# Sparse expert layer by scatter to expert regions and register-addressed block loads, and attention's output projection in plain fp32

## The chip, the cores and the metric

One Trainium2 chip, one core of it. The metric is device time in microseconds (us) of the whole kernel, one launch. In the profile PE is TensorE (matmuls; PEld its weight loads), DVE is VectorE, ACT ScalarE, POOL GpSimd, SP SyncE, which issues the plain DMAs.

## What is computed

Two layers on `x` of 4 sequences x 256 tokens x 256 values. Each layer adds an attention part and a feed-forward part, each on a layer-normed x and scaled by the tanh of a gate. The change touches the second layer only:

```python
# attention, 16 heads, scores against kv_r (4 x 256 x 64)
ctx_c = einsum('bhsl,bld->bhsd', softmax(scores), kv_r)
out = einsum('bhsd,hkd->bshk', ctx_c, w_kc_kv).reshape(...) @ Wo.T
# feed-forward: 16 experts of width 128, two per token, and a shared part
scores = sigmoid(x @ gate_w)
_, selected = top_k(scores + expert_bias, 2)
top = take_along_axis(scores, selected, 1); top = top / top.sum(-1)
y = silu(x @ shared_gate) * (x @ shared_up) @ shared_down
for e in range(16):
    g, u = split(x @ experts_gate_up[e])
    y += comb[:, e] * (silu(g) * u @ experts_down[e])
```

Everything is in fp32. "High and low parts" are a value rounded to fp32r and the rest, also in fp32r: a product is then high x high, high x low and low x high, each a matmul of one pass. A plain fp32 matmul is one instruction in the program; the profile records it as two.

## The kernel before, in words

Each engine has a program of its own, written out by hand; they meet at semaphores only, so the order of the calls in each engine's block (from line 1063 on) is the order of the work. x stays in SBUF as 8 tiles of 128 tokens.

**Attention of the second layer** (`run_pairs`, line 1043) goes over 8 pairs of heads. Each pair has 12 slots; while pair i makes its queries (`q_step`, `rope_step`), pair i-1 makes scores, softmax, values and projection. The folded weights of a pair come from DRAM (`folds`) two pairs ahead, by SyncE (lines 1113 to 1120): `load_folds`, then `load_rope_folds`. ScalarE rounds them (`high_part`, `high_f`) and GpSimd subtracts (`low_part`, `low_f`). For each of 4 sequences b, in slots 5, 7, 9 and 11: `values` (slot 2b+4) leaves a sum in bank 7, ScalarE copies it as c_h (`values_high`), VectorE subtracts for c_l (`values_low`), and one slot later `project` (line 1362) does six fp32r matmuls of 128x256 against f_h and f_l. VectorE's `add` puts the result onto x. After pair 7 comes a last round of slots without queries.

**Between attention and the sparse layer.** Hooks in the slots of that last round begin the next norm: slots 8 to 10 do the norm of the first half (tiles 0 to 3) and its transposes, slot 11 runs `attention_to_ffn` (line 1408) on TensorE ahead of that slot's own `project`: router logits of the first half, their transposes, and the first gate-up of the shared feed-forward. ScalarE's `route_first_half` is in the same slot. Then both halves: statistics, scaling, transposes, logits, `choose1` (two best experts of each token as one-hots), `rank_pe` (line 475: rank of each token within its expert, by matmuls with a triangle of ones), and `place` (line 495): from the ranks the slot of each of the 2048 choices in a compact list in which each expert fills whole blocks of 128 rows, then for each of 31 blocks the rows that it holds, by 16 one-hot matmuls (`rows_pe1`, line 487) of `spread` and `in_blk`. `owners` (line 529) gives each block's expert as a column offset into the weights. The shared part (`ffn1`) is woven in between.

**The blocks** (class `Blocks`, line 817). SyncE stores the normed x twice as `xn_rows` in DRAM; GpSimd gathers the 128 rows of each block into one of four `moe_x` tiles by an indirect DMA (`gather`, line 823), waiting on the turn of the block four before. TensorE turns the tile, does gate-up (line 863) and down (line 882) in plain fp32 with weights at an address from a register; the registers of four blocks are loaded ahead of each fourth gate-up (lines 895 to 900), with a limit test at run time. ScalarE and VectorE work between; SyncE stores each block's result as `y_rows` (line 840). When all 31 are stored, GpSimd gathers from them by 16 indirect DMAs (`fetch`, line 830) each token's two results, and `combine` (line 960) adds them onto x, weighted. Four stores of 256 KB end the kernel. TensorE starts the blocks when both halves of the shared part are added to x (`ffn1.acc` at 2, line 1428).

## Time and profile before

| | us |
|---|---|
| median of 3 runs | 642.78 |
| lowest, highest | 639.86, 644.35 |
| the profiled execution, its own time | 644.12 |
| its span, first to last instruction | 642.3 |
| PE, DVE, ACT, POOL busy | 539.5, 433.3, 293.1, 158.2 |

The first layer ends near 235 us; pairs run to about 478, the last round of slots to 509, routing to 551, blocks to 611.5, and the end is at 642.3. Busy time of PE counts overlapping matmuls with ends that are modelled. A row of the chain gives start, length and what ran; it was found by going back from the last instruction to whatever released it. In brackets behind a timeline's row stands how long the engine was idle ahead of it, and who ended that.

### The profile page before, as it was taken

Reading aid. Unit: us, or ns where it says so; the run is one execution under the profiler, and the core shown is the slowest. Engines: PE = TensorE matmul, PEld = TensorE weight load, DVE = VectorE, ACT = ScalarE, POOL = GpSimd, SP = SyncE. Lnnn points to the kernel's source line nnn. Section 1 sums busy time; section 2 is a strip of 40 time slices with the busy share of each in tenths; the row PEclk is TensorE's granted clock in tenths of the full one; section 3 lists DMA queues with packets and bytes.
Section 4 is the critical chain, followed back from the end, with each engine's and each line's share of the span. In section 5 each row is a group of like instructions: output and inputs, shape, how many; then the busy total and the mean of one; then the engine's idle time right before and its main releaser. Section 6 shows DMA issues by size and latency. Waiting matters only on the chain.

```text
span 642.3 us, 9412 instructions
## 1 busy us (share of the span) xinstructions
PE 539.5 (84%) x2822; PEld 392.2 (61%) x2822; DVE 433.3 (67%) x1152; ACT 293.1 (46%) x753; POOL 158.2 (25%) x161
## 2 busy tenths in 40 slices
PE   6797999987889989999999999999988672799900
PEld 3574687764678865666666666666656442677700
DVE  5997289985465656979787979797878557322213
ACT  3844433335365523545554655464547340255400
POOL 1043156642245512101010101010000011455254
PEclk9868899997889999999999999999998856699965
DMA  7669022221313220101010101000045110134233
GB/s 261 206 225 337 21 73 74 75 66 36 113 35 98 82 82 25 34 26 35 24 33 24 33 24 33 24 0 1 1 180 229 65 66 3 47 112 127 75 106 115
DMA packets 25440, 51.80 MB, mean 81 GB/s; under 512 B 4211, under 2 KB 15421, under 8 KB 25024
## 3 DMA queue, kind: packets, MB, share of 16 engines
q1 hardware_dynamic: 23152, 47.20, 22.2%
q0 software_dynamic: 2256, 4.20, 2.5%
q8 instruction: 16, 0.26, 0.2%
q14 instruction: 16, 0.13, 0.1%
HBM read 40.63 MB, written 12.71 MB: 83 GB/s over the span
## 4 chain that ended last, share of the span: by engine, by line
PE 63%; DVE 19%; ACT 7%; issue 6%; DMA 2%; POOL 2%; POOLq 0%; DVEq 0%; SPq 0%; ACTq 0%
PE bank L1306 10%; PE bank L1324 9%; PE bank L696 8%; PE bank L870 5%; PE bank L1347 5%; PE bank L1357 3%; PE bank L721 3%; DVE left L1704 3%; PE bank L1374 2%; PE bank L886 2%; DVE best L1699 2%; PE bank L1205 2%; PE bank L1338 2%; PE bank L1214 2%; PE bank L374 1%
## 5 line engine op out<-in xcount | busy, mean ns | idle before, releaser
L1522 ACT ACTIVATE silu<-bank,negm 128x256 f32<-128x256 f32 x128 | 59.4, 473 | 37.5 <-DVE negm L1751 37.3
L1530 ACT ACTIVATE probsT<-bank 128x512 f32<-128x512 f32 x64 | 38.4, 600 | 60.9 <-PE bank L1347 60.9
L1324 PE MATMUL bank<-qr,att_w_raw 128*64 128x512 f32 (+1 forms) x192 | 61.9, 605 | 1.2 <-issue 1.2
L1168 POOL TENSOR_TENSOR att_w_l<-att_w_raw,att_w_h 128x384 fp32r<-128x384 f32 x16 | 16.2, 1020 | 167.0 <-ACT att_w_h L1546 167.0
L618 POOL TENSOR_TENSOR ffn_w_l<-ffn_raw,ffn_w_h 128x512 fp32r<-128x512 f32 x30 | 38.7, 1290 | 72.0 <-ACT ffn_w_h L630 57.1
L642 ACT ACTIVATE hid_h<-hid 128x512 fp32r<-128x512 f32 x30 | 18.9, 631 | 67.8 <-DVE hid L657 48.4
L1759 DVE TENSOR_SCALAR hid<-silu,rden 128x256 f32<-128x256 f32 x128 | 47.6, 414 | 2.3
L1347 PEld LDWEIGHTS bank<-ident,hid 128*128 128x128 f32 x256 | 29.2, 142 | 28.3 <-issue 19.2
L1347 PE MATMUL bank<-ident,hid 128*128 128x128 f32 x256 | 40.8, 283 | 5.6 <-DVE hid L1759 2.8
L1751 DVE TENSOR_REDUCE negm<-bank 128x2 f32<-128x512 f32 x64 | 43.6, 682 | 2.2 <-PE bank L1339 1.3
L624 POOL TENSOR_TENSOR ffn_w_l<-ffn_raw,ffn_w_h 128x256 fp32r<-128x256 f32 x30 | 22.9, 765 | 88.4 <-ACT ffn_w_h L634 88.4
L696 PE MATMUL bank<-xT_h,ffn_w_h 128*128 128x512 f32 x120 | 44.2, 454 | 0.0
L826 POOL DMA_INDIRECT moe_x<-xn_rows,route_rows x31 | 31.1, 1004 | 43.3 <-DVE route_rows L545 16.9
L696 PE MATMUL bank<-xT_l,ffn_w_h 128*128 128x512 f32 x120 | 41.8, 432 | 0.0
L1770 DVE SCALAR_TENSOR_TENSOR x<-bank,tg,x 128x512 f32<-128x512 f32 x32 | 23.8, 744 | 21.5 <-PE bank L1374 21.5
L1338 PE MATMUL bank<-ks_h,qs 128*128 128x256 f32 x128 | 36.9, 310 | 1.6 <-ACT silu L1522 1.6
L721 PE MATMUL bank<-ffn_w_h,hid_h 128*128 128x256 f32 x120 | 31.5, 294 | 7.9 <-DVE x L673 4.4
L870 PE MATMUL bank<-moe_w,moe_xT 128*128 x124 | 34.5, 403 | 3.9 <-issue 2.4
L1737 DVE TENSOR_TENSOR qr<-bank,cosq 128x512 f32<-128x512 f32 x48 | 33.0, 687 | 5.0 <-PE bank L1306 4.6
L655 DVE TENSOR_TENSOR silu<-silu,bank 128x512 f32<-128x512 f32 x22 | 15.1, 686 | 31.3 <-ACT rows L447 16.5
L951 DVE COPY moe_hidT<-bank 128x128 f32<-128x128 f32 x31 | 9.0, 292 | 39.3 <-PE bank L879 39.3
L1357 PE MATMUL bank<-probsT,kv 128*64 128x256 f32 x256 | 35.4, 398 | 0.0
(217 smaller groups left out, 1357.9 us busy)
## 6 DMA issues: line engine op xcount, KB each, us to landing
ffn_raw<-in_w_ffn SPq DMA_DIRECT2D x30, 256.0 KB, 2.6
pair_w<-in_pair_w SPq DMA_DIRECT2D x8, 768.0 KB, 5.6
moe_w<-in_w_moe SPq DMA_DIRECT2D x2, 3072.0 KB, 14.0
folds<-att_w_raw SPq DMA_DIRECT2D x6, 896.0 KB, 6.8
att_w_raw<-folds SPq DMA_DIRECT2D x12, 384.0 KB, 3.1
y_rows<-moe_y SPq DMA_DIRECT2D x31, 128.0 KB, 1.8
ffn_raw<-in_w_ffn SPq DMA_DIRECT2D x30, 128.0 KB, 2.3
xn_rows<-xn SPq DMA_DIRECT2D x4, 512.0 KB, 3.5
```

Of the source, the lines that this page charges most:

```text
L618: nc.gpsimd.tensor_tensor(wt_l[b][:, 0:GU], raw[b][:, 0:GU], wt_h[b][:, 0:GU], ALU.subtract).then_inc(self.wgl, 1)
L696: last = nc.tensor.matmul(bank[2 * st.b + g][:], wp[st.b][:, (2 * kt + g) * P:(2 * kt + g + 1) * P], xp[:, kt, st.hf * 512:(st.hf + 1) * 512],
L721: last = nc.tensor.matmul(bank[4 + t // 2][:, (t % 2) * D:(t % 2 + 1) * D], hp[st.b][:, t * P:(t + 1) * P], wp[st.b][:, GU:WC], start=(sel ...
L870: last = nc.tensor.matmul(bank[2 + b % 2][:, 0:2 * P], xgT[b % 2][:, k, :], cells[:, bass.ds(cell + k * 2 * P, 2 * P)], start=(k == 0), st ...
L1306: last = nc.tensor.matmul(bank[bk][:], m_of(wp[b], k, j), xp[:, k, c * 512:(c + 1) * 512], start=(m == 0), stop=(m == 5))
L1324: last = nc.tensor.matmul(bank[2][cols, :], g_of(w_raw[b], 2 * j + w)[:, cols], qr[n % JT][:, w, :], start=(first and w == 0), stop=(not f ...
L1338: nc.tensor.matmul(o, q, ks_h[:, keys], start=True, stop=False)
L1347: last = nc.tensor.matmul(bank[6][:, (2 * h + k) * P:(2 * h + k + 1) * P], pn[u % 2][:, h, k * P:(k + 1) * P], ident[:], start=True, stop= ...
L1357: last = nc.tensor.matmul(bank[7][h * C:(h + 1) * C, 0:S], kv[:, 2 * b + k, 0:C], pT2[b % 2][:, h, k, :], start=(k == 0), stop=(k == 1), s ...
L1522: last = nc.scalar.activation(ex[u % 2][:, h, :], bank[4 + u % 2][:, h * S:(h + 1) * S], ACT.Exp, bias=negm[:, u % 2, h:h + 1], accum_out= ...
L1751: nc.vector.tensor_reduce(negm[:, u % 2, :], bank[4 + u % 2][:].rearrange("p (h n) -> p h n", h=2), AX_X, ALU.max, negate=True).then_inc(s ...
L1759: last = nc.vector.tensor_scalar(pn[u % 2][:, h, :], ex[u % 2][:, h, :], rden[:, u % 2, h:h + 1], None, ALU.mult)
```

## The change

1. **Projection.** c and f are kept in fp32 as they are. Per sequence: two fp32 matmuls instead of six fp32r; `values_low` on VectorE and `low_f` on GpSimd are gone.
2. **Order at the end of attention.** TensorE's hook of slot 11 goes behind the slots. ScalarE does the root of the second half before the logits of the first. Ranks, and slots made from them, come in two halves.
3. **Scatter in.** `xn_slots` in DRAM has 1024 rows for each of 16 experts. GpSimd scatters each of the 8 tiles of normed x twice, straight from SBUF, to row expert x 1024 + rank: 16 indirect DMAs. All of `xn_slots` (16.8 MB) is first set to zero by 8 DMAs of SyncE, two ahead of the pairs and one in each of the six passes that load folds. The stores of `xn_rows` go.
4. **Blocks in.** SyncE loads each block of 128 rows by a plain DMA whose row is in a register (four loaded at a time); `owners` makes these rows too.
5. **Blocks out.** GpSimd scatters each block's result to `y_rows`, ordered by choice and token; rows that hold no token get an index past the end. SyncE then reads all back by 8 plain DMAs of 256 KB, where 16 gathers stood.
6. **Registers.** No limit test at run time; loaded ahead of the turn of a block instead of ahead of its gate-up. The expert weights come as one DMA of 6 MB instead of two.
7. `place` builds `spread` as one operation instead of 16, and the row sum is in bf16 over two tables (`blk_val`).

```diff
                 def project(j, jb, b):
                     if b == 0:
-                        pe.wait_ge(s_fl, j + 1)
+                        pe.wait_ge(s_fc, j + 1)
                     pe.wait_ge(s_xa, j * 4 + (b + 1))
-                    for part, fps in ((c_h, (f_h, f_l)), (c_l, (f_h,))):
-                        if part is c_h:
-                            pe.wait_ge(s_ch, j * 4 + (b + 1))
-                        else:
-                            pe.wait_ge(s_cl, j * 4 + (b + 2))
-                        for t in range(2):
-                            for fp in fps:
-
-                                last = nc.tensor.matmul(bank[3][:, t * D:(t + 1) * D],
-                                                        part[b % 2][:, t * P:(t + 1) * P], fp[jb][:],
-                                                        start=(t == 0 and part is c_h and fp is f_h),
-                                                        stop=(part is c_l), skip_group_check=True)
+                    pe.wait_ge(s_c, j * 4 + (b + 2))
+                    for t in range(2):
+                        last = nc.tensor.matmul(bank[3][:, t * D:(t + 1) * D], cv[b % 2][:, t * P:(t + 1) * P],
+                                                fo[jb][:], start=True, stop=True)
                     last.then_inc(s_y, 1)
...
-                def attention_to_ffn():
-                    route[1][0].pe_logits(pe)
-                    route[1][0].pe_turn_logits(pe)
-                    ffn1.gateup(pe, ffn1_first)
                 run_pairs(slot, pe, {Q3_AT - 1: lambda: n_att[1].pe_transpose(pe),
                                      Q3_AT: lambda: n_att[1].pe_whole(pe)},
-                          {10: lambda: n_ffn1[0].pe_transpose(pe), 11: attention_to_ffn})
-                pe.wait_ge(route[1][0].act, 1)
-                pe.wait_ge(s_xa, NPAIR * B + 1)
+                          {10: lambda: n_ffn1[0].pe_transpose(pe)})
+                route[1][0].pe_logits(pe)
+                route[1][0].pe_turn_logits(pe)
+                ffn1.gateup(pe, ffn1_first)
...
+                rank_pe(pe, 0)
                 route[1][1].pe_logits(pe)
                 route[1][1].pe_turn_logits(pe)
+                pe.wait_ge(s_slot, 1)
+                rank_pe(pe, 1)
                 ffn1.gateup(pe, ffn1_second)
-                pe.wait_ge(ffn1.hid, 1)
-                rank_pe(pe)
                 ffn1.pe_down(pe, ffn1_first)
                 rows_pe1(pe)
                 ffn1.pe_down(pe, ffn1_second)
-                pe.wait_ge(s_row_of, 1)
...
+                    clear_slots(i)
                 with sp.Fori(0, (NPAIR - 2) // 2) as ii:
                     for b in range(2):
 
                         sp.wait_ge(s_wl, ii * (2 * WPARTS) + WPARTS * (b + 1))
-                        sp.wait_ge(s_fl, ii * 2 + (b + 1))
+                        sp.wait_ge(s_fc, ii * 2 + (b + 1))
                         load_folds(ii * 2 + (b + 2), b)
                         sp.wait_ge(s_rp, ii * (4 * JT) + 2 * JT * (b + 1))
                         load_rope_folds(ii * 2 + (b + 2), b)
+                        clear_slots(ii * 2 + b)
...
+                sp.dma_start(cells[:], a["w_moe1"]).then_inc(s_cell, 16)
+                blocks.prog_sp(sp)
...
+        def slots(dve, seq, hf):
+
+            ts = slice(4 * hf, 4 * hf + 4)
+            dve.wait_ge(s_rank, hf + 1)
             dve.wait_ge(s_cst, 16)
-            ranks = bank[0][:, 0:NT * E1].rearrange("p (t e) -> p t e", e=E1)
-            count = bank[0][:, NT * E1:(NT + 1) * E1]
+            seq.link(nc.vector.tensor_tensor(
+                capv[:, ts, :], ranks[hf][:, 0:4, :],
+                cst[:, C_CAP:C_CAP + E1].unsqueeze(1).broadcast_to([P, 4, E1]), ALU.add))
+            seq.link(nc.vector.tensor_tensor(
+                smul[:, ts, :, :], ohs[:, ts, :, :], capv[:, ts, :].unsqueeze(2).broadcast_to([P, 4, 2, E1]),
+                ALU.mult))
+            cs = slice(8 * hf, 8 * hf + 8)
+            seq.link(nc.vector.tensor_reduce(slot_of[:, cs], smul[:, ts, :, :].rearrange("p t j e -> p (t j) e"),
+                                             AX_X, ALU.add))
+            nc.vector.tensor_copy(slot_u[:, cs], slot_of[:, cs]).then_inc(s_slot, 1)
...
+        def owners(seq):
+
+            one, n = slice(0, 1), NBLK
+            g = cst[one, C_SUB:C_SUB + n]
+            seq.link(nc.vector.tensor_tensor(ends[:], base[one, :], nblk[one, :], ALU.add))
+            seq.link(nc.vector.tensor_tensor(
+                below[:], ends[:].unsqueeze(1).broadcast_to([1, n, E1]),
+                g.unsqueeze(2).broadcast_to([1, n, E1]), ALU.is_le))
+            seq.did(nc.vector.tensor_reduce(owner[:], below[:], AX_X, ALU.add))
+            seq.link(nc.vector.tensor_tensor(
+                taken[:], below[:], nblk[one, :].unsqueeze(1).broadcast_to([1, n, E1]), ALU.mult))
+            seq.link(nc.vector.tensor_reduce(first_of[:], taken[:], AX_X, ALU.add))
+            seq.link(nc.vector.tensor_tensor(first_of[:], g, first_of[:], ALU.subtract))
+            seq.link(nc.vector.tensor_scalar(first_of[:], first_of[:], float(P), None, ALU.mult))
+            seq.link(nc.vector.scalar_tensor_tensor(out=row_f[:], in0=owner[:], scalar=float(T), in1=first_of[:],
+                                                    op0=ALU.mult, op1=ALU.add))
+            seq.did(nc.vector.tensor_scalar(row_at[:], row_f[:], float(E1 * T - P), None, ALU.min))
+            seq.link(nc.vector.tensor_scalar(cell_at[:], owner[:], float(E1 - 1), float(CELL), ALU.min,
+                                             ALU.mult))
+            nc.vector.tensor_copy(owner[:], row_f[:]).then_inc(s_owner, 1)
+
...
+            seq.did(nc.vector.tensor_reduce(blk_of[:], reach[:, :, 1:NBLK + 1], AX_X, ALU.add))
+            seq.link(nc.vector.tensor_tensor(in_blk[:], reach[:, :, 0:NBLK], reach[:, :, 1:NBLK + 1],
+                                             ALU.subtract))
+            seq.did(nc.vector.tensor_tensor(
+                blk_val[:], in_blk[:].unsqueeze(2).broadcast_to([P, 2 * NT, 2, NBLK]),
+                cst[:, C_VAL:C_VAL + 4 * NT].rearrange("p (c v) -> p c v", v=2).unsqueeze(3).broadcast_to(
+                    [P, 2 * NT, 2, NBLK]), ALU.mult))
             seq.link(nc.vector.scalar_tensor_tensor(out=lane[:], in0=blk_of[:], scalar=-float(P), in1=slot_of[:],
                                                     op0=ALU.mult, op1=ALU.add))
-            for c in range(2 * NT):
-                last = nc.vector.tensor_scalar(spread[:, c, :], cst[:, C_LANE:C_LANE + P], lane[:, c:c + 1],
-                                               cst[:, C_ROW + c:C_ROW + c + 1], ALU.is_equal, ALU.mult)
-            last.then_inc(s_spread, 1)
-
-        def owners(seq):
-
-            one = slice(0, 1)
-            seq.link(nc.vector.tensor_tensor(ends[:], base[one, :], nblk[one, :], ALU.add))
-            seq.link(nc.vector.tensor_tensor(
-                below[:], ends[:].unsqueeze(1).broadcast_to([1, NBLK, E1]),
-                cst[one, C_BLK:C_BLK + NBLK].unsqueeze(2).broadcast_to([1, NBLK, E1]), ALU.is_le))
-            seq.link(nc.vector.tensor_reduce(owner[:], below[:], AX_X, ALU.add))
-            nc.vector.tensor_scalar(owner_i[:], owner[:], float(E1 - 1), float(CELL), ALU.min,
-                                    ALU.mult).then_inc(s_owner, 1)
+            nc.vector.tensor_tensor(
+                spread[:], cst[:, C_LANE:C_LANE + P].unsqueeze(1).broadcast_to([P, 2 * NT, P]),
+                lane[:].unsqueeze(2).broadcast_to([P, 2 * NT, P]), ALU.is_equal).then_inc(s_spread, 1)
 
...
         class Blocks:
 
-            def clear(self, pool):
-                for i in range(NGB):
-                    nc.gpsimd.memset(xg[i][:], 0.0).then_inc(s_xg0, 1)
-
-            def gather(self, pool, b):
-                if b >= NGB:
-                    pool.wait_ge(s_mt, b - NGB + 1)
+            def place(self, pool, hf):
+
+                pool.wait_ge(s_clr, 16 * CLEARS)
+                pool.wait_ge(s_slot, hf + 1)
+                for t in range(4 * hf, 4 * hf + 4):
+                    for c in (2 * t, 2 * t + 1):
+                        nc.gpsimd.indirect_dma_start(
+                            xn2, bass.IndirectOffsetOnAxis(ap=slot_u[:, c:c + 1], axis=0), xn[:, t, :], None,
+                            bounds_check=E1 * T - 1, oob_is_err=False).then_inc(s_xsc, 16)
+
+            def scatter(self, pool, b):
+                pool.wait_ge(s_my, b + 1)
                 nc.gpsimd.indirect_dma_start(
-                    xg[b % NGB][:], None, xn2, bass.IndirectOffsetOnAxis(ap=rows_u[:, b:b + 1], axis=0),
-                    bounds_check=2 * T - 1, oob_is_err=False).then_inc(s_xg[b % NGB], 16)
-
-            def fetch(self, pool):
-                for i in range(NYB):
-                    pool.wait_ge(s_ysc[i], 16 * len(range(i, NBLK, NYB)))
-                for t in range(NT):
-                    for j in range(2):
-                        nc.gpsimd.indirect_dma_start(
-                            yback[j][:, t, :], None, y2,
-                            bass.IndirectOffsetOnAxis(ap=slot_u[:, 2 * t + j:2 * t + j + 1], axis=0),
-                            bounds_check=NBLK * P - 1, oob_is_err=False).then_inc(s_back[t // 2], 16)
-
-            def store(self, sp, b):
-                sp.wait_ge(s_my, b + 1)
-                sp.dma_start(y2[b * P:(b + 1) * P, :], ysb[b % NYB][:]).then_inc(s_ysc[b % NYB], 16)
+                    y2, bass.IndirectOffsetOnAxis(ap=rows_u[:, b:b + 1], axis=0), ysb[b % NYB][:], None,
+                    bounds_check=2 * T - 1, oob_is_err=False).then_inc(s_ysc[b % NYB], 16)
 
             def prog_pool(self, pool):
+                self.place(pool, 0)
+                self.place(pool, 1)
                 pool.wait_ge(s_row_of, 1)
-                pool.wait_ge(s_xg0, NGB)
-                pool.wait_ge(s_xrow, 64)
-                for b in range(NGB):
-                    self.gather(pool, b)
-                for b in range(NBLK - NGB):
-                    self.gather(pool, b + NGB)
-                self.fetch(pool)
+                for b in range(NBLK):
+                    self.scatter(pool, b)
+
+            def values(self, eng, at, b, top):
+                n = min(4, NBLK - b)
+                _, got = nc.values_load_multi_w_load_instructions(
+                    at[0:1, b:b + n], engines=[eng], min_val=0, max_val=top,
+                    skip_runtime_bounds_check_because="the value is held under its limit by the minimum before it")
...
+                pe.wait_ge(s_cell, 16)
                 pe.wait_ge(s_owner, 1)
-                cell = {}
+                cell = self.values(mybir.EngineType.PE, cell_at, 0, (E1 - 1) * CELL)
                 self.turn(pe, 0)
                 self.turn(pe, 1)
                 for b in range(NBLK + 2):
-                    if b % 4 == 0 and b < NBLK:
-                        n = min(4, NBLK - b)
-                        _, got = nc.values_load_multi_w_load_instructions(
-                            owner_i[0:1, b:b + n], engines=[mybir.EngineType.PE], min_val=0,
-                            max_val=(E1 - 1) * CELL)
-                        cell.update({b + i: v for i, v in enumerate(got)})
                     if b < NBLK:
                         self.gateup(pe, b, cell[b])
                     if 1 <= b <= NBLK:
                         self.turn_hidden(pe, b - 1)
                     if b >= 2:
                         self.down(pe, b - 2, cell[b - 2])
+                    if b % 4 == 3 and b + 1 < NBLK:
+                        cell.update(self.values(mybir.EngineType.PE, cell_at, b + 1, (E1 - 1) * CELL))
                     if b + 2 < NBLK:
                         self.turn(pe, b + 2)
...
             def finish_sp(self, sp):
-                for b in range(NBLK):
-                    self.store(sp, b)
+                for i in range(NYB):
+                    sp.wait_ge(s_ysc[i], 16 * len(range(i, NBLK, NYB)))
+                for g in range(NT // 2):
+                    for j in range(2):
+                        sp.dma_start(yback[j][:, 2 * g:2 * g + 2, :],
+                                     y2[j * T + 2 * g * P:j * T + 2 * (g + 1) * P, :].rearrange(
+                                         "(t p) d -> p t d", p=P)).then_inc(s_back[g], 16)
...
                 dve.wait_ge(s_xa, NPAIR * B + 1)
+                dve.wait_ge(s_rp, NPAIR * 2 * JT)
                 n_ffn1[1].stats(seq)
+                n_ffn1[1].scale(dve, seq)
                 choose1(route[1][0], dve, seq)
-                n_ffn1[1].scale(dve, seq)
                 n_ffn1[1].low(dve)
+                slots(dve, seq, 0)
                 choose1(route[1][1], dve, seq)
+                slots(dve, seq, 1)
+                compact(dve, seq)
                 ffn1.hidden(dve, ffn1_first)
+                owners(seq)
                 ffn1.low(dve, nc.vector, ffn1_first)
                 place(dve, seq)
                 ffn1.hidden(dve, ffn1_second)
+                ffn1.add(dve, ffn1_first)
                 rows_of(dve, seq)
-                owners(seq)
                 ffn1.low(dve, nc.vector, ffn1_second)
-                ffn1.add(dve, ffn1_first)
                 ffn1.add(dve, ffn1_second)
                 pick_weights(seq)
                 blocks.prog_dve(dve)
                 dve.wait_ge(ffn1.acc, 2)
                 blocks.combine(dve, seq)
```

## Rows read from the trace of the kernel before

**Rows 1.** Page, section 4: the chain by engine.

```profile
PE 63%; DVE 19%; ACT 7%; issue 6%; DMA 2%; POOL 2%; POOLq 0%; DVEq 0%; SPq 0%; ACTq 0%
```

**Rows 2.** Four stretches (columns stand in the first line).

```profile
core 0: us, PE busy (x) PEld busy (x) DVE busy (x) ACT busy (x) POOL busy (x), PEclk, DMA share, GB/s
372.00:406.00 34.00, 33.62 (x193) 22.56 (x194) 28.48 (x62) 19.62 (x57) 3.50 (x4) 1.00 0.09 27
520.00:550.00 30.00, 15.95 (x71) 12.35 (x69) 18.02 (x62) 6.02 (x9) 5.94 (x9) 0.61 0.07 20
550.00:613.00 63.00, 55.69 (x279) 44.44 (x279) 18.03 (x72) 29.45 (x93) 26.92 (x27) 0.94 0.31 94
613.00:642.00 29.00, 0.00 (x0) 0.00 (x0) 6.71 (x16) 0.00 (x0) 16.25 (x16) 0.54 0.38 109
```

**Rows 3.** Timeline of VectorE, additions into x one pair apart (start us, us, engine, line).

```profile
400.00 0.74 DVE L1770 SCALAR_TENSOR_TENSOR x<-bank,tg,x 128x512 f32<-128x512 f32 x1
...
431.73 0.74 DVE L1770 SCALAR_TENSOR_TENSOR x<-bank,tg,x 128x512 f32<-128x512 f32 x1
```

**Rows 4.** Chain in order of time (start us, us, what): attention, then block loop.

```profile
410.73 0.71 PE bank L1374 x6
...
570.58 0.86 PE bank L870 x4
...
571.56 0.43 PE bank L886 x2
```

**Rows 5.** Chain, last pair.

```profile
487.85 0.42 DVE c_l L1765
```

**Rows 6.** Timeline of VectorE around the last projection (in brackets: idle before, releaser).

```profile
503.62 0.42 DVE L1765 TENSOR_TENSOR c_l<-bank,c_h 128x256 fp32r<-128x256 f32 x1 [0.83 <-ACT c_h L1536]
509.48 0.75 DVE L1770 SCALAR_TENSOR_TENSOR x<-bank,tg,x 128x512 f32<-128x512 f32 x1 [5.43 <-PE bank L1374]
```

**Rows 7.** Timeline of TensorE, transposes of the second half.

```profile
516.23 1.94 PE L323 MATMUL bank<-ident,xn 128*128 128x128 f32 x8 [6.79 <-DVE xn L308]
```

**Rows 8.** Timeline of VectorE in routing.

```profile
531.97 0.69 DVE L515 TENSOR_TENSOR route_reach<-route_slot,route_const 128x512 f32<-128x512 f32 x1
...
534.28 4.19 DVE L525 TENSOR_SCALAR route_spread<-route_const,route_lane 128x128 fp32r<-128x128 f32 x16
...
542.15 0.17 DVE L543 CAST route_slot_at<-route_slot 128x16 uint32<-128x16 f32 x1 [3.09 <-PE bank L491]
...
549.49 1.66 DVE L673 SCALAR_TENSOR_TENSOR x<-bank,tg,x 128x256 f32<-128x256 f32 x4 [3.02 <-PE bank L721]
```

**Rows 9.** Timeline of GpSimd, one gather of a block.

```profile
545.05 1.00 POOL L826 DMA_INDIRECT moe_x<-xn_rows,route_rows  x1 [0.30 <-issue]
```

**Rows 10.** Chain in the block loop, two gate-ups behind register loads.

```profile
568.70 1.13 PE bank L870 x4
...
575.88 1.12 PE bank L870 x4
```

**Rows 11.** Timeline of all engines at the end.

```profile
611.16 0.38 ACT L927 ACTIVATE moe_y<-bank 128x256 f32<-128x256 f32 x1 [0.21 <-PE bank L886]
...
633.76 1.22 POOL L835 DMA_INDIRECT moe_back<-y_rows,route_slot_at  x1 [0.30 <-issue]
637.76 0.88 DVE L964 SCALAR_TENSOR_TENSOR x<-xn,pick_weight,x 128x256 f32<-128x256 f32 x2 [3.65 <-DMA moe_back<-y_rows,route_slot_at]
```

**Rows 12.** Stretch in which xn is stored in rows of 1 KB (columns as in rows 2).

```profile
502.00:504.00 2.00, 2.00 (x12) 0.72 (x9) 1.07 (x2) 0.45 (x2) 0.00 (x0) 0.79 1.04 348
```

**Rows 13.** Timeline: a load of folds issued, and ScalarE's first touch of it.

```profile
267.97 0.33 SPq L1094 DMA_DIRECT2D att_w_raw<-folds  x1
...
295.55 0.53 ACT L1546 ACTIVATE att_w_h<-att_w_raw 128x384 fp32r<-128x384 f32 x1
```

**Rows 14.** Timeline of VectorE and GpSimd: a cast beside a memset.

```profile
525.93 0.69 DVE L466 CAST idxf<-idx 128x8 f32<-128x8 uint32 x1
...
525.53 1.06 POOL L821 MEMSET moe_x<- 128x256 f32 x4
```

195 lines of the change are left out of this document (97 added, 98 removed).

## Prediction

> **What bounds the kernel now.** I read the page's shares of the chain first, then the stretches, then the chain and the timelines of the two places that the change touches. TensorE holds 63% of the chain, VectorE 19% [rows 1]. In attention TensorE is the bound: in 34 us of steady pairs it is busy 33.62 us at full clock [rows 2], and a pair takes 431.73 - 400.00 = 31.7 us, read at the same addition into x one pair apart [rows 3]. So TensorE time added there is paid in full. In the routing from 520 to 550 us this no longer holds: TensorE is busy 15.95 of 30 us, at a clock of 0.61 of full, and VectorE 18.02 us [rows 2]; it is a relay between engines. From 550 to 613 us TensorE is the bound again (55.69 of 63 us), and in the last 29 us it has no work at all: GpSimd issues 16 gathers [rows 2].
>
> The profiled execution took 644.12 us with a span of 642.3; the median of the three runs is 642.78. I sum against the span and take the same difference off the median.
>
> **1. Projection.** Before, one sequence's projection is six high-and-low matmuls and holds the chain for 0.71 us [rows 4]. After, it is two plain fp32 matmuls of 128x256. That form stands in the trace: the sparse layer's down product is one fp32 matmul of 128x256, recorded as two pieces, 0.43 us; its gate-up product is two of them, 0.86 us at full clock [rows 4]. So a projection costs 0.86 - 0.71 = +0.15 us. It runs 32 times; 28 lie in the seven pairs that TensorE bounds: +4.3 us. Bounds: 0 if the four VectorE subtractions per pair that go (c_l, 0.42 us) opened as much room on TensorE, and +8 if half of what a product pays after an idle queue (1.12 for 0.86, [rows 4, 10]) came on top of each. TensorE idles only 0.4 us in those 34 us [rows 2], so little room can open; I take +4.3.
>
> In the last pair there is no projection of queries to fill TensorE, and the chain goes through ScalarE and VectorE: c_h, then c_l 0.42 us [rows 5], then the next maximum. Three such c_l leave the chain: -1.2 us (bounds 0 and -1.7). Of the copies of f, ScalarE's stays and GpSimd's subtraction goes: it lay beside a busy TensorE, so 0.
>
> **2. The last projection no longer waits for router and gate-up.** Before, the tail hook puts logits, their turning and the first gate-up of the shared tile ahead of the fourth projection; VectorE starts c_l at 503.62 and after it idles 5.43 us, until x is added at 509.48 [rows 6]. After, the projection comes straight behind c (c_l started when ScalarE's copy was there, so 503.6) and takes 0.9 us, or 1.7 at half clock: the addition starts near 504.9, 4.6 us earlier. Late next is what stood in front. TensorE still owes those 5.4 us of work, now from 504.9 on, and ScalarE copies the logits only behind the root of the second half, which waits for the statistics; I allow 2.2 us for that. So TensorE's transposes of the second half start at 512.5 instead of 516.23 [rows 7], 3.7 us earlier. (xn is there before: the transposes began 6.75 us behind the addition [rows 6, 7], with the first half's choice, about 2.2 us of VectorE, in between, and that now stands behind the scaling: 504.9 + 4.6 = 509.5.) The experts of the second half were chosen 11.1 us behind the start of those transposes: the casts of their choice start at 525.93 [rows 14], and 1.35 us later that choice is done, at 527.28. One table load of ScalarE goes from this stretch, as the root now comes before both sigmoids; I take 1.3 us for it: chosen at 512.5 + 9.7 = 522.2.
>
> **3. Routing on VectorE.** From 522.2: rank 0.6, slots 4 small operations 1.1 (523.9), compact 1.5 (four operations as L502 to L508), hidden 0.7, owners eleven operations. Prices by size: 16 elements a partition 0.17, 512 elements 0.69 [rows 8], so 1.05 ns an element on top (128 elements 0.29, 256 elements 0.42). Owners: three of 496 elements plus one reduction 2.7, seven small ones 1.3, gaps 0.2: 4.2, done at 530.3. Low 0.6. Place: eight operations, two of them larger than any shown: blk_val 992 elements 1.2, spread as one operation of 2048 elements 0.69 + 1536 x 0.00105 = 2.3, where sixteen took 4.19 [rows 8]; sum 7.5, done at 538.4. The sixteen matmuls that sum the rows become bf16 and fall under the first addition of the shared tile (1.65). Hidden 0.6, addition 1.6, rows 0.7, low 0.6, the second down product, addition 1.66: acc reaches 2 at 545.3, where it stood at 551.15 before (549.49 + 1.66 [rows 8]). TensorE waits for that and for nothing later, so blocks start 5.8 us earlier. Bounds: -2 (every new operation 30% dearer, transposes only 2 us earlier) and -9.
>
> What is queued beside it: GpSimd needs the slots of the first half (516.9) and then issues 16 scatters. The trace has no scatter; the nearest row is the gather of 128 rows, 1.00 us with 0.30 between two [rows 9]: 16 x 1.3 = 20.8, last issue at 537.7, landing 2.8 later (from 633.76 + 1.22 to 637.76 [rows 11]), then a plain load of 128 KB, about 2.4: block 0 is in at 542.9, 3.0 us before TensorE asks. Bounds for a scatter: 0.27 us (GpSimd's memset of a tile of this size, 1.06 for four [rows 14]) and 2.3 us (the gather doubled). I take 1.3. Where this cover goes is rival 3.
>
> **4. Block loop.** Per block TensorE holds the chain for 0.86 + 0.43 [rows 4] and about 0.34 of two turns: 1.63 us. Every fourth block costs more, since the registers of the next four are loaded: from one such gate-up to the next 575.88 - 568.70 = 7.18 us, less 4 x 1.63 leaves 0.66, of which 0.26 is a longer first product (1.12 for 0.86) [rows 4, 10]. Seven such: 4.6 us. After, the limit test on each value is gone and the load stands before the turn. Bounds: 0 and -4.6; I take -1.8. GpSimd now issues one scatter a block (1.3 us, under 1.63), SyncE one plain load where it issued one store. A y buffer is free again about 4 us after its copy (1.3 + 2.8) and is wanted after four blocks, 6.5 us. At the head of the loop the registers are now loaded before the first turn, where they were behind it: about 0, within what I took.
>
> **5. End.** Before: last moe_y at 611.16 + 0.38 = 611.54, store, 16 gathers of which the last starts at 633.76 and is awaited until 637.76, addition 1.7, store to 642.3 [rows 11]: 30.8 us. After: scatter starts 0.5 later and takes 1.0, lands 2.8 later (615.8); then eight plain loads, 2.1 MB in rows of 1 KB. The nearest rows are the stores of xn, also rows of 1 KB, at 348 GB/s [rows 12]: 6.1 us, plus about 2.4 to the first byte and receipt: 624.3. Addition of the last group 1.7, store 2.9: 628.9. The gain is 13.4 us. Bounds -5 (150 GB/s) and -16.
>
> **6. Clears.** Eight DMAs write 16.8 MB of zeros, two before the pairs and one in each of six pairs, behind the loads of folds in SyncE's queue. At 345 GB/s one takes 6.1 us. The loads of folds that go out at 267.97 are first touched by ScalarE at 295.55 [rows 13]: 27.6 us of cover, and the DMA engines are 9% busy there [rows 2]. Cost 0; if one clear took over 28 us, every pair would wait.
>
> Sum: +4.3 - 1.2 - 5.8 - 1.8 - 13.4 = -17.9, span 624.4, median 642.78 - 17.9 = 624.9, so 625.
>
> **Rivals.** (1) The start gains nothing: VectorE's longer list (owners 4.2 for 1.8) eats what part 2 gives. For it: place and owners stand on VectorE before the second hidden; against: the 4.19 of spread halves. 624.9 + 5.8 = 631.
>
> (2) VectorE holds GpSimd up. The cast at L466 took 0.69 us beside a GpSimd memset [rows 14], and the cast of twice as many elements at L543 took 0.17 [rows 8], so the two do block each other. If the scatters waited for VectorE's busy 60% of that stretch (18.02 of 30 us [rows 2]), some 12 us would be added, block 0 would be in at 554.9 and TensorE would start 9 late: 634. Against it: the gather at 545.05 took the usual 1.00 us [rows 9] while VectorE subtracted and added (its addition runs from 544.83). The Trainium skill, page "SBUF — State Buffer", section "Who interferes with whom", says that copies, casts and tensor_scalar on VectorE can lock the port pair that it shares with GpSimd, while tensor_tensor takes only the read side. By that rule only a handful of small operations in the window block, under 1 us; the cast agrees.
>
> (3) Slower than before: a scatter costs GpSimd far more than a gather. With 1.3 + z us each, the start is later by 16z - 3.0, and beyond z = 0.43 GpSimd also bounds the loop, by 31(z - 0.43). All 17.9 us are gone at 47z = 34.2, z = 0.73, a scatter of 2.0 us. At 2.3 (z = 1): 624.9 + 13 + 17.7 = 656. For it: nothing in the trace is a scatter, and GpSimd's margin in the loop is only 0.33 us; against: gathers for the blocks and for the return take 1.0 to 1.2 us alike [rows 9, 11].
>
> (4) The rows come back no faster than the gathers did, 150 GB/s: 14 instead of 6.1 us, 633.
>
> (5) Clears go far slower than 345 GB/s and hold the folds: at 30 us each some 2 us a pair, 637, and more beyond.
>
> **Chances.** Forecast 0.60, rival 1 0.12, rival 2 0.07, rival 4 0.09, rival 3 0.08, rival 5 0.04. Faster by over 1% (about what a measurement here can tell): 0.60 + 0.12 + 0.07 + 0.09 = 0.88; within 1%: 0.02, half of rival 5; slower: 0.08 + 0.02 = 0.10. The range 616 to 636 takes in rivals 1, 2 and 4 and, below, the loop's other end (-2.8), the start at -9 (-3.2) and projection at 1 instead of 4.3.
>
> **What would show it.** Right: steady pairs of 32.3 us; x added near 505; blocks start near 546; seams of 0.4 us in the loop; one landing group after another from 618 and 17 us from last moe_y to the end. Wrong: a first turn that waits for a moe_x load (GpSimd's stream too slow), GpSimd scatters over 1.6 us, TensorE waiting for att_w_h, pairs no longer than 31.7.

## Result and the profile after

| | before | after |
|---|---|---|
| median of the runs beside each other (4 and 4) | 641.32 | 613.46 |
| lowest, highest | 639.40, 644.35 | 610.86, 615.70 |
| the profiled execution | 644.12, span 642.3 | 611.38, span 609.2 |

The ratio is 0.956, 95% interval 0.949 to 0.963: 27.9 us faster. The forecast was 625.0 with a range from 616 to 636, a gain of 17.9; the median lies 2.5 us under the range. The changed kernel run again (`a0_again`, below) gave a ratio of 0.955 (0.949 to 0.962), and the median of all its ten runs is 615.6, a gain of 26; that is 0.4 us under the range. So the sign was right and some 8 to 10 us of gain were not foreseen. One execution each of `a0_again` (620.4) and `a5_spread_in_sixteen` (621.4) lies over 1.5% above the fastest of its kernel and is left out of their ratios; without it their medians are 615.6 and 612.5 instead of the 616.6 and 615.8 given below.

To find them I cut each profile at the same events: the first addition of attention into x, the 25th (six pairs later), the 32nd and last, the end of the last addition of the shared part (acc at 2), the first turn of a block, the end of the last moe_y (a block's result, copied by ScalarE), the end of the span. In us:

| stretch | before | after | again | forecast | measured |
|---|---|---|---|---|---|
| to the first addition | 272.6 | 267.8 | 270.2 | 0 | -4.8, -2.4 |
| six pairs | 190.9 | 193.0 | 193.0 | +3.6 | +2.1 |
| last pair's rest and last round | 46.0 | 38.2 | 38.2 | -5.2 | -7.8 |
| routing, to acc at 2 | 41.7 | 38.5 | 38.5 | -1.3 | -3.1 |
| acc to the first turn | 0.2 | 0.7 | 0.7 | 0 | +0.5 |
| blocks | 60.2 | 53.6 | 55.2 | -1.8 | -6.6, -5.0 |
| last moe_y to the end | 30.8 | 17.4 | 17.7 | -13.4 | -13.3, -13.0 |

(The forecast's column is the prediction's sum laid out by these events: 24 projections of 0.15, then 0.6 - 1.2 - 4.6, then 545.3 - 504.9 against 551.15 - 509.48. It adds up to -18.1 where the prediction has -17.9: its +4.3 is 28 times 0.15, which is 4.2, and the rest is rounding.)

The page's chain by engine, after, beside [rows 1]:

```profile
PE 61%; DVE 13%; issue 8%; POOL 6%; ACT 6%; DMA 3%; SPq 0%; DVEq 0%; POOLq 0%; ACTq 0%
```

Four stretches of the same parts as [rows 2], same columns (pairs, routing, blocks, end):

```profile
372.00:406.00 34.00, 33.70 (x183) 21.97 (x182) 24.76 (x53) 19.16 (x54) 2.01 (x2) 1.00 0.27 89
520.00:550.00 30.00, 18.59 (x100) 15.18 (x100) 19.66 (x52) 7.05 (x20) 14.26 (x13) 0.76 0.32 100
550.00:592.00 42.00, 41.20 (x224) 33.99 (x222) 12.50 (x51) 23.63 (x75) 25.21 (x26) 1.00 0.38 113
592.00:609.00 17.00, 0.00 (x0) 0.00 (x0) 6.51 (x16) 0.00 (x0) 1.95 (x2) 0.62 0.55 185
```

VectorE's share of the chain fell from 19% to 13%. In the blocks TensorE is now busy 41.20 of 42 us where it was 55.69 of 63. The two rows don't cover the same part: that of before holds the start of the loop at a low clock, that of after begins behind it. What went are mostly the pauses; the table of the loop below takes this apart. From the last moe_y to the end, without TensorE work, it is 17.4 us instead of 30.8. VectorE's additions one pair apart, as in [rows 3]:

```profile
396.45 0.74 DVE L1788 SCALAR_TENSOR_TENSOR x<-bank,tg,x 128x512 f32<-128x512 f32 x1
...
428.62 0.74 DVE L1788 SCALAR_TENSOR_TENSOR x<-bank,tg,x 128x512 f32<-128x512 f32 x1
```

A pair is 32.17 us, up from 31.73 in [rows 3] and from 31.8 on average over the six. The projection itself, in the chain (as L1374 x6 in [rows 4]): 

```profile
395.21 0.86 PE bank L1404 x4
400.62 0.99 PE bank L1404 x4
```

The end, timeline of all engines, as in [rows 11]:

```profile
591.39 0.38 ACT L974 ACTIVATE moe_y<-bank 128x256 f32<-128x256 f32 x1 [0.22 <-PE bank L936]
592.18 0.97 POOL L876 DMA_INDIRECT y_rows<-moe_y,route_rows  x1 [0.30 <-issue]
593.46 0.98 POOL L876 DMA_INDIRECT y_rows<-moe_y,route_rows  x1 [0.30 <-issue]
595.68 0.39 SPq L1026 DMA_DIRECT2D xn<-y_rows  x1
...
599.15 0.88 DVE L1011 SCALAR_TENSOR_TENSOR x<-xn,pick_weight,x 128x256 f32<-128x256 f32 x2 [8.64 <-DMA moe_back<-y_rows]
...
605.48 0.87 DVE L1016 SCALAR_TENSOR_TENSOR x<-moe_back,pick_weight,x 128x256 f32<-128x256 f32 x2
```

Last moe_y ends at 591.77. GpSimd still has the scatter of the block before to issue (592.18), since at the end results come faster than its 1.28 us a scatter; the last one starts at 593.46. 2.2 us later SyncE issues the loads, and from 599.15 on VectorE adds, with one gap of 0.69 us. That is the forecast's 17 us from last moe_y to the end.

### The profile page after: what moved, and what is told of

Its sections match the earlier page's. It is cut to its first block, busy times and chain, and to the rows that moved or that the text cites. A ratio compares the mean times of both kernels' runs of the same rounds, so it can differ in the third digit from the quotient of the medians.

```text
span 609.2 us, 9266 instructions
## 1 busy us (share of the span) xinstructions
PE 529.5 (87%) x2762; PEld 381.6 (63%) x2762; DVE 423.0 (69%) x1122; ACT 289.9 (48%) x751; POOL 152.2 (25%) x150
## 4 chain that ended last, share of the span: by engine, by line
PE 61%; DVE 13%; issue 8%; POOL 6%; ACT 6%; DMA 3%; SPq 0%; DVEq 0%; POOLq 0%; ACTq 0%
PE bank L1342 10%; PE bank L1360 9%; PE bank L741 9%; PE bank L1393 5%; PE bank L1383 5%; PE bank L1404 4%; POOL y_rows L876 4%; PE bank L766 3%; DVE left L1727 3%; PE bank L1374 3%; DVE best L1722 2%; POOL xn_slots L870 2%; PE bank L1375 2%; PE bank L1241 2%; PE bank L1250 2%
## 5 line engine op out<-in xcount | busy, mean ns | idle before, releaser
L1555 ACT ACTIVATE probsT<-bank 128x512 f32<-128x512 f32 x64 | 38.3, 599 | 66.2 <-PE bank L1383 66.2
L1782 DVE TENSOR_SCALAR hid<-silu,rden 128x256 f32<-128x256 f32 x128 | 45.2, 395 | 2.3
L741 PE MATMUL bank<-xT_h,ffn_w_h 128*128 128x512 f32 x120 | 42.1, 434 | 0.0
L1760 DVE TENSOR_TENSOR qr<-bank,cosq 128x512 f32<-128x512 f32 x48 | 33.1, 689 | 12.0 <-PE bank L1342 11.9
L1374 PE MATMUL bank<-ks_h,qs 128*128 128x256 f32 x128 | 39.0, 327 | 1.8 <-ACT silu L1547 1.8
L870 POOL DMA_INDIRECT xn_slots<-xn,route_slot_at x16 | 17.6, 1100 | 82.4 <-DVE route_slot_at L524 77.8
L876 POOL DMA_INDIRECT y_rows<-moe_y,route_rows x31 | 30.1, 970 | 30.3 <-issue 18.7
L741 PE MATMUL bank<-xT_h,ffn_w_l 128*128 128x512 f32 x120 | 36.0, 425 | 0.0
L1360 PEld LDWEIGHTS bank<-qr,att_w_raw 128*64 128x64 f32 (+1 forms) x192 | 18.8, 153 | 26.0 <-issue 23.8
L1404 PE MATMUL bank<-att_f,c 128*128 128x256 f32 x128 | 33.8, 386 | 1.2 <-ACT c L1561 1.2
## 6 DMA issues: line engine op xcount, KB each, us to landing
moe_w<-in_w_moe SPq DMA_DIRECT2D x1, 6144.0 KB, 17.8
```

The source lines that it names most:

```text
L741: last = nc.tensor.matmul(bank[2 * st.b + g][:], wp[st.b][:, (2 * kt + g) * P:(2 * kt + g + 1) * P], xp[:, kt, st.hf * 512:(st.hf + 1) * 512],
L876: nc.gpsimd.indirect_dma_start(y2, bass.IndirectOffsetOnAxis(ap=rows_u[:, b:b + 1], axis=0), ysb[b % NYB][:], None, bounds_check=2 * T - 1 ...
L1360: last = nc.tensor.matmul(bank[2][cols, :], g_of(w_raw[b], 2 * j + w)[:, cols], qr[n % JT][:, w, :], start=(first and w == 0), stop=(not f ...
L1374: nc.tensor.matmul(o, q, ks_h[:, keys], start=True, stop=False)
L1404: last = nc.tensor.matmul(bank[3][:, t * D:(t + 1) * D], cv[b % 2][:, t * P:(t + 1) * P], fo[jb][:], start=True, stop=True)
L1782: last = nc.vector.tensor_scalar(pn[u % 2][:, h, :], ex[u % 2][:, h, :], rden[:, u % 2, h:h + 1], None, ALU.mult)
```

## Experiments

Labels with p start from the kernel before, with a and b from the changed one. All medians of one batch are read against the kernel before on the same chip. The diffs here are in short, not line for line.

### The parts alone: projection, order

`p1_projection`: the kernel before with the fp32 projection only. `p2_order`: before with the order at the end of attention only. `a1_projection_back`: the changed kernel with the six-matmul projection of before.

```diff
 # p1                                     # p2
-  6 matmuls c_h,c_l x f_h,f_l (fp32r)    -  {10: ..., 11: attention_to_ffn}  (tail hooks, TensorE)
+  2 matmuls c x f (fp32)                 +  {10: ...}; attention_to_ffn()    (behind the last slot)
-  values_low, low_f                      -  choose1(first half) ahead of scale(second half)
                                          +  scale(second half) ahead of choose1(first half)
```

> The kernel before with the projection alone in plain fp32 (c and f kept whole, c_l and f_l gone). Forecast's theory: +0.15 us a projection in the steady pairs, -1.2 us in the last round, in all +3 us. Clock theory (the profile of after kept TensorE at full clock in the last round, where before fell to 0.72 from 482 to 488 us): the fp32 projection holds the clock up, the last round is then some 3 us shorter than in before, in all 0 or below. Steady pair: 32.1 us as in after (0.35 more than 31.75) under both.

> The kernel before with the order at the end of attention alone changed: last projection ahead of logits, turning and gate-up; root and scaling of the second half first. Forecast: the last addition into x 4.6 us earlier, of which 3.4 to 3.7 arrive at the chosen experts and at the start of the blocks. Rival (relay late elsewhere: gate-up still stands ahead of the transposes of the second half): under 1.5 us arrive.

> The kernel after with the projection in high and low parts again. Forecast: steady pairs back at 31.75 us, last round 1.2 us longer, in all 3 us faster than after. Clock theory: TensorE falls to half clock in the last round again, which gets some 3 us longer, so the whole is no faster than after.

| | median, ratio (95%) | six pairs | last round | routing |
|---|---|---|---|---|
| before | | 190.9 | 46.0 | 41.7 |
| p1_projection | 637.7, 0.995 (0.992 to 0.998) | 193.0 | 43.4 | 41.7 |
| p2_order | 638.2, 0.995 (0.992 to 0.999) | 191.1 | 41.3 | 40.6 |
| a1_projection_back | 614.9, 0.957 (0.952 to 0.963) | 190.9 | 41.3 | 38.5 |
| changed | 613.5, 0.956 (0.949 to 0.963) | 193.0 | 38.2 | 38.5 |

The projection costs 2.1 us in six pairs wherever it is, and gives back 2.6 (in before) to 3.2 us (in the changed kernel) in the last round; net that is about 1 us at most, less than the medians can show (614.9 with the old projection, 613.5 and 616.6 with the new). The order gives 4.7 us there, as forecast (4.6), and 1.1 more in routing: 5.8 us arrive at the start of the blocks, where 3.4 to 3.7 were expected. In the last round the two add up: 2.6 + 4.7 = 7.3 of 7.8. The medians of these two don't follow the stretches closely: 3.6 and 3.2 us under before, where the stretches from the first addition on say 0.1 and 5.4; the stretch ahead of it, below, moves by several us from profile to profile (4.7 between before and p1_projection). The projection's 2.6 comes together with a higher granted clock: over the whole stretch before had 0.93, p1_projection 1.00, and the kernel changed has 1.00 where a1_projection_back has 0.92. How much of the 2.6 is the clock and how much the three c_l that left the chain no run separates. The stretch 470 to 490 us (columns as in [rows 2]), before and then p1_projection:

```profile
470.00:490.00 20.00, 16.87 (x103) 12.13 (x102) 13.34 (x33) 11.37 (x35) 0.00 (x0) 0.91 0.79 323
```

```profile
470.00:490.00 20.00, 16.99 (x108) 12.12 (x106) 14.21 (x35) 13.42 (x44) 0.00 (x0) 1.00 0.80 327
```

### The pauses in the block loop

```diff
 # a2_limit_test (after): TensorE's register loads with the limit test again, at the new place
 # p3_no_limit_test (before): the test gone, the load where it stood
 # a3_load_place (after): no test, the load ahead of each fourth gate-up again
-  if b % 4 == 3 and b + 1 < NBLK: cell.update(self.values(...))     # behind down, ahead of turn(b + 2)
+  if b % 4 == 0 and 0 < b < NBLK: cell.update(self.values(...))     # a3, ahead of gateup(b)
   values_load_multi_w_load_instructions(..., max_val=...,
+      skip_runtime_bounds_check_because=...)          # p3, at the old place; a2 takes it away
```

> The kernel after with the limit test at run time back on TensorE's register loads, at their new place (SyncE's stay without). If the test made the seam of 0.66 us in every fourth block, the loop is 2 to 4.6 us longer than in after, with seams of 0.3 to 0.66 us; if the place made it, the period stays 1.63 us a block.

> The kernel before, with one edit: TensorE's register loads without the limit test at run time; they stand where they stood, ahead of each fourth gate-up. If the test makes the whole loss at every fourth block: first turn to last moe_y 54 instead of 60.2 us, blocks evenly 1.63 apart, 635.5. If the place before the gate-up makes it: no change, 641.3. If the test is half of it: 638.

> The changed kernel with the register loads of TensorE put back ahead of each fourth gate-up, still without the limit test. If the test alone made the loss: blocks evenly 1.63 apart, no change to the changed kernel (615.5). If the place matters too: 0.2 to 0.4 us at each of seven gate-ups, 1.5 to 3 us longer.

| | median | acc to first turn | blocks |
|---|---|---|---|
| before: test, ahead of gate-up | 641.3 | 0.2 | 60.2 |
| p3_no_limit_test | 637.1, 0.989 (0.983 to 0.996) | 0.2 | 55.5 |
| changed: no test, ahead of turn | 613.5 | 0.7 | 53.6 |
| a2_limit_test | 617.9 (one run) | 1.9 | 59.7 |
| a3_load_place | 614.4, 0.958 (0.951 to 0.965) | 0.7 | 53.8 |

The chain of p3_no_limit_test in the loop, one block and its neighbours:

```profile
565.16 0.43 PE bank L886 x2
565.59 0.22 PE bank L859 x2
565.81 0.87 PE bank L870 x4
...
567.44 0.87 PE bank L870 x4
...
569.07 0.86 PE bank L870 x4
...
570.69 0.86 PE bank L870 x4
```

Every gate-up here is 1.63 us behind the last, over the place where the registers are loaded too. The chain of a2_limit_test has the pause at every fourth:

```profile
553.37 0.43 PE bank L937 x2
553.80 0.41 issue
554.21 0.41 PE bank L912 x2
554.62 0.94 PE bank L921 x4
...
556.33 0.86 PE bank L921 x4
...
560.56 0.43 PE bank L937 x2
560.99 0.46 issue
561.46 0.41 PE bank L912 x2
```

"issue" is time in which TensorE waited for nothing that the profile shows. Here it is the test: 0.4 us of issue, twice as long a turn (0.41 for 0.22), a longer gate-up. Restored it costs 6.1 us of blocks and 1.3 ahead of the first turn; taken from the kernel before it gives 4.7. These two numbers, and 60.2 against 53.6, hold more than the test. Taken apart at the first, fourth and last gate-up:

| | acc to first gate-up | first to fourth gate-up | fourth to last (27 blocks) | from there to last moe_y |
|---|---|---|---|---|
| before | 2.21 | 6.00 | 48.55 | 3.63 |
| p3_no_limit_test | 1.53 | 6.46 | 44.05 | 3.63 |
| a2_limit_test | 3.16 | 6.11 | 48.70 | 3.63 |
| changed | 1.88 | 4.99 | 43.73 | 3.63 |
| its repeat | 1.89 | 6.63 | 43.72 | 3.63 |
| a3_load_place | 1.88 | 5.00 | 43.90 | 3.63 |

The 27 blocks behind the fourth gate-up run at full clock in all of them. There the seven tests cost 4.5 us (before against p3_no_limit_test) to 5.0 (a2_limit_test against changed), 0.64 to 0.71 each. The place is worth 0.2 to 0.3 us in all, at the last of the seven loads. So four register loads alone pass nearly unseen behind the queue of matmuls, and four tests do not. The first four gate-ups differ by the clock granted there: from the first turn to the fourth gate-up it was 0.62 in before, 0.74 in after and 0.58 in its repeat. In this order:

```profile
551.36:559.36 8.00, 7.09 (x26) 5.49 (x27) 2.72 (x12) 2.38 (x8) 3.69 (x4) 0.62 0.13 35
```

```profile
538.21:544.41 6.20, 6.18 (x26) 4.68 (x27) 2.29 (x11) 2.37 (x8) 0.00 (x0) 0.74 0.41 114
```

```profile
540.56:548.40 7.84, 7.71 (x26) 6.01 (x27) 2.28 (x11) 2.39 (x8) 0.00 (x0) 0.58 0.28 92
```

What TensorE did ahead of that is the same routing relay in after and its repeat. So of the 6.6 us by which the blocks are shorter in after, 4.8 are the seven tests and the place, 0.8 the very first register load (0.7 of it its test; the load itself now stands ahead of the first turn, outside this stretch), and 1.0 goes with the clock; in the repeat the clock took 0.6 us back.

### The way back

```diff
 # a6_gathers_back (after, old way back)      # p4_scatter_back (before, new way back alone)
-  GpSimd scatters each moe_y                 -  SyncE stores each moe_y; 16 gathers at the end
-  8 plain loads at the end                   +  GpSimd scatters each moe_y, between its gathers
+  SyncE stores each moe_y; 16 gathers        +  8 plain loads at the end
```

> The changed kernel with the old way back: SyncE stores each block as it comes, and after the last one GpSimd gathers 16 times 128 rows; nothing else is undone. If the end's gain is all from this: last moe_y to the end 30.8 instead of 17.4, the loop and all before it as in the changed kernel, 626.8. If the scatters also cost the loop something, the loop falls under 53.5. If SyncE, which now loads and stores, holds TensorE: turns wait for moe_x, the loop over 54.5.

> The kernel before with the new way back alone: each block's result is scattered by GpSimd as it comes and eight plain loads bring the rows back; the gathers of the blocks stay with GpSimd. If GpSimd's stream bounds the loop (one gather and one scatter a block, 2 x 1.27 = 2.55 us against 1.63): first turn to last moe_y about 31 x 2.55 = 79 instead of 60.2 us, the end 17.5 instead of 30.8, together +5.5: 647, slower than before. If the two overlap better than they were issued alone: loop 60 to 65, 629 to 634. The register test is still in.

a6_gathers_back: 625.4 (ratio 0.973, 0.968 to 0.979). From last moe_y to the end 31.3 us instead of 17.4, blocks 53.8: the gain at the end is this edit, and SyncE carries loads and stores without holding TensorE. The median rose by 9 to 12 us only, against 616.6 in the same batch and 613.5. Its profile reached the first addition at 264.9, earlier than any other, and took 0.8 us longer in the last round and 1.9 longer in routing. The edit adds one small copy to those parts; the granted clock was lower in both (0.83 for 0.91 in 490 to 510 us, and 0.56 for 1.00 in the stretch 24 to 28 us behind the last addition).

p4_scatter_back: 656.5, ratio 1.022 (1.015 to 1.028), slower than before; whether by over 2% is open. The end is 19.0 us, but the blocks take 90.1 instead of 60.2. GpSimd's timeline there:

```profile
583.16 1.03 POOL L826 DMA_INDIRECT moe_x<-xn_rows,route_rows  x1 [0.30 <-issue]
584.49 1.02 POOL L832 DMA_INDIRECT y_rows<-moe_y,route_rows  x1 [0.31 <-issue]
585.81 1.03 POOL L826 DMA_INDIRECT moe_x<-xn_rows,route_rows  x1 [0.30 <-issue]
589.61 1.02 POOL L832 DMA_INDIRECT y_rows<-moe_y,route_rows  x1 [2.76 <-ACT moe_y L923]
```

Gather and scatter take 2.66 us a block together, over TensorE's 1.63: 31 times that is 82.5 us, where 79 were expected. On top GpSimd stands still six times in the loop, for 1.8 to 3.0 us each, mostly waiting for a moe_y; its program takes gathers and scatters in turn, so the next gather waits too. With both the blocks take 90. So the regions per expert, which let SyncE fetch a block by one plain load, are what makes the scatter of the results affordable.

### The clears

`a4_clears_twice`: each of the eight clears issued twice, the extra one into a tensor that nothing reads.

> The changed kernel with each of the eight clears issued twice, the second into a tensor that nothing reads: 33.6 MB of zeros instead of 16.8. If the clears are hidden behind the pairs, as forecast (27.6 us of cover for 6.1 us, now 12 to 16): pairs stay at 32.17 us, no change. If a clear takes most of its cover: ScalarE waits for att_w_raw and pairs get longer by several us each.

Six pairs take 193.0 us, as with single clears: hidden, with as much again to spare. From the end of the first layer to the first addition it took 38.3 us where every kernel with this projection and single clears (or none: p1_projection) took 37.7, so the doubled clears ahead of the pairs may cost 0.5 us; the single ones cost nothing there. Its time was 620.8, one run, nearly all of the difference ahead of the first addition (276.7), which leads to the next point.

### The stretch that nothing touched

`a0_again`: the changed kernel, unchanged.

> The changed kernel itself, unchanged, a second time. Three profiles of kernels with the plain fp32 projection reached the first addition into x at 266.2 to 267.9 us, three with high and low parts at 272.0 to 272.6, though both run the same code until 235 us. If that is drawn anew with each execution (the granted clock), this profile may show anything from 266 to 273, and the single times spread over 5 us or more; if it belongs to the kernel, it shows 267 to 268 again and the median stays at 613.5 within 1.5. Steady pairs 32.2, blocks 53.6 from first turn to last moe_y, 17.4 from there to the end in both.

616.6 (610.6 to 620.4), first addition at 270.2. The kernels run the same code up to 235 us, and their profiles end it anywhere between 227.2 (a6_gathers_back) and 238.4 us (a4_clears_twice); after had 230.1, its repeat 232.4, before 235.2. What differs in them is the granted clock. The stretch 60 to 80 us (columns as in [rows 2]) in before:

```profile
60.00:80.00 20.00, 17.99 (x79) 12.59 (x78) 6.80 (x28) 9.67 (x22) 5.74 (x4) 0.76 0.25 91
```

in after:

```profile
60.00:80.00 20.00, 17.99 (x84) 13.25 (x84) 8.07 (x29) 10.34 (x23) 7.07 (x5) 0.85 0.25 94
```

and in its repeat:

```profile
60.00:80.00 20.00, 17.99 (x78) 13.02 (x78) 6.53 (x28) 9.88 (x23) 5.80 (x4) 0.76 0.24 92
```

TensorE is equally busy in all three, and gets 79, 84 and 78 groups of its instructions done. Over all 17 profiles the end of the first layer follows the clock granted up to it: 227.2 to 228.8 us at a mean of 0.95 (six profiles), 230.1 to 231.0 at 0.94 (four), 232.4 to 234.9 at 0.92 (four), 235.2 and 235.4 at 0.91, 238.4 at 0.89. Over the whole span four of the repeat's six runs show the same: 610.6 us at 0.949, 611.3 at 0.945, 615.6 at 0.935, 620.4 at 0.923, and the other two lie between.

Does the change itself move that clock? By the single profiles it might: ten of the eleven kernels with the fp32 projection reached the first addition at 264.9 to 270.2 us, and five of the six with high and low parts at 272.0 to 273.9. The exceptions are a4_clears_twice (276.7) and p4_scatter_back (267.6). The medians speak against it: if the changed kernel were faster there by 4.8 us, they would differ by 33 us like the profiles, and they differ by 26 to 28, what the other stretches give. The profile of before was simply one of its slower runs (644.1, median 641.3), that of after one of the faster (611.4, median of ten 615.6). I read the 4.8 us of this stretch as not the change's; p1_projection, whose median gained 3.6 us where its later stretches give 0.1, keeps that open for a part. The change's own part of the difference between the two profiles is 33.1 - 4.8 = 28.3 us, and 28.8 - 2.4 = 26.4 against the repeat.

### What holds the first block

The forecast had block 0 loaded 3.0 us before TensorE asks. In after, the chain ran through the scatters and that load, as if they held the start. The timeline of GpSimd and VectorE, then the chain:

```profile
526.24 0.97 POOL L870 DMA_INDIRECT xn_slots<-xn,route_slot_at  x1 [0.30 <-issue]
...
527.09 1.19 DVE L574 TENSOR_TENSOR route_blk_val<-route_in_blk,route_const 128x992 bf16<-128x992 f32 x1
527.52 1.61 POOL L870 DMA_INDIRECT xn_slots<-xn,route_slot_at  x1 [0.30 <-issue]
...
528.40 2.29 DVE L580 TENSOR_TENSOR route_spread<-route_const,route_lane 128x2048 bf16<-128x2048 f32 x1
...
529.43 2.11 POOL L870 DMA_INDIRECT xn_slots<-xn,route_slot_at  x1 [0.31 <-issue]
```

```profile
536.04 1.99 DMA moe_x<-xn_slots
538.03 0.18 issue
538.21 1.19 PE bank L911 x4
```

Fourteen of 16 scatters cost 0.97 to 1.18 us. The two beside VectorE's widest operations took 1.61 and 2.11 and ended 0.85 us behind them (529.13 against 528.28, 531.54 against 530.69). Three kernels change only those operations, and `b2_pieces_queues` cuts both in pieces and issues half of the eight loads at the end from ScalarE.

```diff
 # a5: spread by 16 tensor_scalar   # a7: by 4 tensor_tensor of 512   # a8: tensor_tensor to fp32, then a copy
-  nc.vector.tensor_tensor(spread[:], ..., ALU.is_equal)      # 2048 elements, bfloat16
+  for c in range(16): nc.vector.tensor_scalar(spread[:, c, :], ...)                        # a5
+  for c in range(0, 16, 4): nc.vector.tensor_tensor(spread[:, c:c + 4, :], ...)            # a7
```

> The changed kernel with spread made by sixteen tensor_scalar operations instead of one tensor_tensor of 2048 elements. By the rows, 16 x 0.26 = 4.2 us instead of 2.3, so acc reaches 2 about 1.9 later and the first turn too: 617.4. In the changed kernel the two scatters beside blk_val and spread took 1.61 and 2.11 us instead of 0.97. If wide tensor_tensor operations hold GpSimd up, only the scatter beside blk_val stays long here and the stream ends 1.1 us earlier. If it is tensor_scalar that takes the port, as the Trainium skill says, the scatters beside the sixteen get longer than 2.1. If the length comes from the scatter itself, nothing changes in them.

> The changed kernel with spread made by four tensor_tensor operations of 512 elements instead of one of 2048. So far a scatter that met blk_val or spread ended 0.85 us after that operation ended, in each of three profiles, so it seems to wait for its end. If what matters is how long one operation holds: the scatter beside the four takes at most 1.5 instead of 2.11 us, the stream of scatters ends 0.6 to 1.1 earlier, and the first turn comes straight behind acc (0.67 to about 0.2). If any bfloat16 tensor_tensor holds GpSimd as long as the stream of them runs: 2.1 again. The time differs from the changed kernel's by less than 1 us either way: 615.5.

> The changed kernel with spread made as fp32 by one tensor_tensor of 2048 elements into a spare tile, and then copied to bfloat16. If length alone stretches the scatter: one beside the fp32 tensor_tensor takes up to 2.1 to 3 us, ending 0.85 behind it. If it is the bfloat16 result: scatters beside the fp32 tensor_tensor stay at 0.97, as they did beside the 512-element fp32 ones, and one beside the copy is long. The copy adds 0.6 to 2.2 us to the start of the blocks.

> The changed kernel with blk_val in two and spread in four operations, and the eight loads at the end issued half by SyncE and half by ScalarE. If both small costs are real: first turn 0.5 earlier, the end 17.0 instead of 17.4 to 17.7, together -1: 614.5; no more than the measurement tells. If the pieces cost more in overheads than the scatters gain: 615.5 to 616.

The timeline of both engines in a5_spread_in_sixteen:

```profile
525.28 1.19 DVE L574 TENSOR_TENSOR route_blk_val<-route_in_blk,route_const 128x992 bf16<-128x992 f32 x1
525.71 1.60 POOL L871 DMA_INDIRECT xn_slots<-xn,route_slot_at  x1 [0.30 <-issue]
...
526.59 3.40 DVE L581 TENSOR_SCALAR route_spread<-route_const,route_lane 128x128 bf16<-128x128 f32 x16
...
527.62 0.97 POOL L871 DMA_INDIRECT xn_slots<-xn,route_slot_at  x1 [0.30 <-issue]
528.90 0.97 POOL L871 DMA_INDIRECT xn_slots<-xn,route_slot_at  x1 [0.30 <-issue]
```

and in a8_spread_f32:

```profile
529.34 2.29 DVE L580 TENSOR_TENSOR moe_back<-route_const,route_lane 128x2048 f32<-128x2048 f32 x1
530.37 2.65 POOL L872 DMA_INDIRECT xn_slots<-xn,route_slot_at  x1 [0.30 <-issue]
...
531.66 1.23 DVE L584 CAST route_spread<-moe_back 128x2048 bf16<-128x2048 f32 x1
```

| | scatters beside blk_val, spread | routing | acc to first turn | median |
|---|---|---|---|---|
| changed | 1.61, 2.11 | 38.5 | 0.67 | 613.5, 616.6 |
| a5_spread_in_sixteen | 1.60, 0.97 | 40.0 | 0.67 | 615.8 |
| a7_spread_in_four | 1.60, 1.11 | 38.7 | 0.68 | 615.4 |
| a8_spread_f32 | 1.60, 2.65 | 39.8 | 0.68 | 614.7 (one run) |
| b2_pieces_queues | 1.08, 1.09 and 1.50 | 38.8 | 0.67 | 613.1 |

For the tensor_tensor it is the length of the one operation that counts, not the bfloat16 result: cut in four it leaves 1.11 of 2.11, and with an fp32 result the scatter is still long. In a8_spread_f32 it ended 1.39 us behind the tensor_tensor (533.02 against 531.63) and not 0.85, so the copy (CAST) that followed from 531.66 on may have held it too. The sixteen tensor_scalar operations left GpSimd alone; whether because they are short or because only one of their inputs is a whole tensor, no run separates.

But the second column from the right says more. Relative to acc, the first block's load went out 1.5 us ahead in after (536.04 against 537.55) and 3.9 us ahead in a5_spread_in_sixteen (533.36 against 537.25), and in between in the others, and acc to first turn stayed at 0.67. So the chain's way through the scatters was a near tie, and what stands in front of the first turn is TensorE's own loading of four registers, now ahead of it: with the limit test on these loads it is 1.92 (a2_limit_test), and in before, where that load came behind the first turns, it was 0.21. b2_pieces_queues is not to be told from the changed kernel (0.959, 0.955 to 0.963), and neither is `b1_mixed`, which keeps high and low parts in pairs 0 to 6, takes fp32 in the last pair only, and issues half of the eight loads from ScalarE:

> The changed kernel with high and low parts in pairs 0 to 6, where TensorE is the bound, plain fp32 only in the last pair, where ScalarE and VectorE are on the chain, and the eight loads at the end issued half by SyncE and half by ScalarE. If the projection's price lies on TensorE and its gain in the last round alone: pairs 31.8 instead of 32.2 (-2.1 in six), last round 38.2 as in the changed kernel, end 16.7 instead of 17.4, together -2.8: 610.7. If the later first addition (272.5) belongs to kernels with high and low parts, 4.7 us come on top: 615.4. If the last round's gain hung on VectorE's room in pairs before it, the last round is 41: 613.5.

615.4 us, ratio 0.955 (0.950 to 0.959). Six pairs were back at 191.1, the end was 17.1, but the last round took 39.2 and routing 39.5, a microsecond more each; the net of about 1 us is under what these runs can tell. Its microsecond in routing, where it has the changed kernel's instructions, goes with a clock of 0.52 for 1.00 in the stretch 24 to 28 us behind the last addition. No version beats the changed kernel by a margin that is shown.

## Why the prediction missed

- **Projection, +4.3.** Each costs 0.86, as forecast. Paid were 2.1 us in 24, 0.09 each instead of 0.15. That the c_l which go open some room on TensorE, the bound named there, would fit; no run shows it by itself.
- **Last round, -1.2 for c_l and -4.6 for the order.** The order was right to 0.1 (p2_order). The c_l were sized too small: with and without the fp32 projection this stretch differs by 2.6 (before) and 3.2 us (changed), where -0.6 was forecast (+0.6 in the last pair, -1.2). I counted three c_l at 0.42 and left the clock out, which rose from 0.93 to 1.00 with them.
- **Routing, -1.3.** Measured -3.1. The single prices held: owners' wide operations 0.66 (0.67), blk_val 1.19 (1.2), spread 2.29 (2.3), scatters 0.97 + 0.30 (1.3). Up to the choice of the second half's experts 0.5 us was forecast and 1.6 came (from the last addition 17.8 us before, 16.2 after). Its transposes began 0.8 us later than forecast, but from there to the choice it took 7.8 us instead of 11.05, with 9.7 forecast: one table load (1.28) went as forecast, the cast at L474 took 0.17 where it was 0.69, and TensorE's transposes and logits ran at full clock where before had half. Before, and then after:

```profile
516.20:522.40 6.20, 4.68 (x14) 2.27 (x14) 1.91 (x4) 1.23 (x3) 0.00 (x0) 0.50 0.50 169
```

```profile
507.40:511.60 4.20, 2.68 (x19) 1.50 (x17) 2.17 (x6) 1.08 (x2) 0.00 (x0) 1.00 0.00 0
```

From the choice to acc 23.9 us became 22.3, with 23.1 forecast.
- **Loop, -1.8 of at most -4.6.** The failed step, and the largest. I had the 0.66 us in [rows 4, 10] right and split it between the test and the load by no row. It was nearly all the test: at full clock, from the fourth gate-up to the last, -4.5 in p3_no_limit_test and +5.0 in a2_limit_test, and -4.8 in the change with the place. The bound of -4.6 was the value to take. The rest of the blocks' -6.6 and -5.0 is the first register load with its test (-0.8) and the clock of the first blocks (-1.0, and +0.6 in the repeat), neither of which the sum had.
- **Head of the loop, "about 0".** +0.5 from acc to the first turn, the register load that now stands there, but -0.8 behind it. From acc to the first gate-up it was 2.21, 1.53 without the test (p3_no_limit_test) and 1.88 with the new place too: the test had cost 0.7 here, the place costs 0.35.
- **End, -13.4.** Measured -13.3 and -13.0. The sum was right, its steps each within about 1 us: the last scatter began 1.7 us behind the last moe_y instead of 0.5, but it had landed after 3.8 instead of 4.3, and from 601.51 on VectorE's additions set the pace and not the loads.
- **Clears, 0.** Right; twice as many were hidden too. Rival 5 falls.
- **Cover of block 0.** Forecast 3.0 (by its own numbers, 545.3 - 542.9, it was 2.4); measured the block was in 0.5 us behind acc and 0.18 ahead of the first turn. Counted from the last addition the block was in 1.0 us later than forecast, the two stretched scatters (+1.8) being in part made good, and acc was 1.9 us earlier. It cost nothing, so rivals 2 and 3 didn't come about: scatters have the gathers' price, and VectorE holds GpSimd up for one operation's length, twice. (Rival 3 counts GpSimd's room in the loop once as 0.43 and once as 0.33 us; 1.63 - 1.3 is 0.33, and with it the gain is gone at z = 0.66 instead of 0.73.) The reason against rival 2 was half wrong: the sentence of the Trainium skill, page "SBUF — State Buffer", section "Who interferes with whom", that tensor_tensor takes only the read side, from which the page infers that the writing of descriptors goes on beside it, does not fit 1.61 and 2.11 us here. The same section says that an operation with two inputs in SBUF contends with a GpSimd instruction that reads SBUF, and that does fit: blk_val and spread have both inputs in SBUF, and each scatter takes its row numbers from route_slot_at, which lies there. The tensor_scalar operations in a5_spread_in_sixteen, which by that section can lock GpSimd out under conditions on their operands, left the scatters at 0.97.
- **Outside the sum.** Of the 33.1 and 28.8 us between the profiles 4.8 and 2.4 come from the stretch before the first addition, by the granted clock; the medians don't have them. Without it the change is worth 26 to 28 us, the other 8 to 10 us being: loop 3.2 to 4.8, last round 2.6, routing 1.8, pairs 1.5, less 0.5 at the head. From the span to the time of the execution it is 2.1 us now and was 1.8, which the forecast took as equal.

The low end of 616 allowed for 9 us: 2.8 in the loop, 3.2 at the start of the blocks, 3.3 in the projection. The loop went past its share, order and routing took 2.0 of theirs and the pairs 1.5, and the last round's c_l, with 1.4 to 2.0 us more than forecast, had no share at all. All four errors point the same way. Those of the last round and of routing came with a higher granted clock, for which the forecast has no term.

## What to carry to other kernels

A run-time limit test on a register value that the matmul engine loads is paid in full in a loop that this engine bounds, here 0.64 to 0.71 us for four values, while the loads themselves pass nearly unseen there; hold the value under its limit where it is computed. Moving the scattered access from the end of a loop into it pays only if the engine that writes the descriptors has the room in every turn: one indirect DMA a block fitted under 1.63 us, two made the kernel slower than before. And where the price of a thing that goes is known but its cause is not, the whole price belongs into the forecast's likely values, not two fifths of it.

## What the runs showed of the hardware that was not expected

- An indirect DMA that GpSimd issues while VectorE works on one long tensor_tensor with both inputs in SBUF ends about 0.85 us behind that operation, instead of after its usual 0.97: 1.61 beside 992 elements, 2.11 beside 2048, 1.08 to 1.50 beside pieces of about 500. It took 2.65 beside 2048 elements with a copy of them right behind, and 0.97 beside tensor_scalar of 128.
- The chain that ended last named the scatters and a load for the first block; having that load go out 2.4 us earlier relative to acc changed nothing. A piece of chain with 0.18 us of slack behind it is a tie.
- A clock drawn anew in each execution moved the same instructions of the first 235 us by up to 11 us between profiles, in step with its mean (0.95 to 0.89), and whole runs of one kernel by 10.
- The way from the first to the fourth gate-up took 4.99 us in one execution of the changed kernel and 6.63 in another, at granted clocks of 0.74 and 0.58 from the first turn on, behind the same instructions. A price read over the whole loop (6.1 and 4.7 for the same test) mixes that in; read over the part at full clock it is 5.0 and 4.5.
